# Row gathers with an explicit index bound and skipping, in a two-layer graph network on one core

## Chip, cores and metric

The kernel runs on one core of a Trainium2 chip. The metric is the device time of one execution in microseconds (us), lower is better. TensorE is called PE in the rows (PEld is its weight load), VectorE DVE, ScalarE ACT, GpSimd POOL and SyncE SP.

## What is computed

Two graph layers on 6,250 nodes of 256 features and 206,250 directed edges sorted by destination. The first one is the part that gathers:

```python
h = relu(layernorm(x))
h_all = einsum('ni,roi->rno', h, weight)            # 8 relations
x = x + segment_sum(h_all[edge_type, src], dst) + bias
h = relu(layernorm(x))
hw = h @ W
out = segment_sum(dinv[src] * dinv[dst] * hw[src], dst) + b
x = x + leaky_relu(out, 0.2)
```

The kernel sums the rows `h[src]` per destination and relation first and multiplies by the relation's weights afterwards, which is the same sum in another order.

## The kernel before

**Prologue.** The rows of `h` are written to `table0` in HBM, 50 tiles of 128 rows (6,400 rows; node i is row i + 64, the rest are padding). The edges are laid out in chunks of 128: `idxT` holds one column of 128 source rows for every chunk, one index per partition. An index is a source node plus 64, so the largest is 6,313; a padded place holds 64. A count of edges that fit the fast layout is compared with E, and the fast path, `both_layers`, runs; the other path, `aggregate_any`, is not executed with these inputs.

**First layer.** A chunk is fetched by one indirect DMA on GpSimd (L1116): 128 rows of 1 KB from `table0` into `rows`. Three chunks make a lot, 538 lots in all (1,612 chunks), and `rows` is a ring of `RING0` = 7 lots. In `sum_lot`, TensorE waits until a lot's rows have landed and multiplies them with one-hot matrices that ScalarE makes (L1657, 12 matmuls for a lot); its last matmul raises `s_pe`, and GpSimd waits on that before it issues the gathers of the lot seven later. After every tile come the projections by the relation weights (L1673).

**Between the lots.** A plan written into the program gives TensorE other work after each lot: counts of edges for the second layer (L1687, up to some 1,300 us), and the dense products of the second layer (L1719). ScalarE and VectorE prepare their operands. GpSimd's queue holds little besides the row gathers: `look` (one gather of `records` at L1097, behind a wait of its own at L1096) and `fetch` (four gathers at L1104), seven times each, and at the end 46 direct DMAs that add to the output (L1125). So GpSimd's order is a single stream of 1,647 indirect DMAs, 1,612 of them of rows.

Of the kernel before, what the change touches and what calls it, by code (L numbers as in the profile page):

```python
# [4 lines left out]
P = 128  # L5
LOT = 3
# [796 lines left out]
def both_layers(nc, D, V):  # L803
# [5 lines left out]
    R, NB, DF, DF3, T, SEGS = D.rel, D.nb, D.d, 3 * D.d, D.tiles, D.segs  # L809
# [10 lines left out]
    idxT, iota, iota4, ident, identb, dinv, ps_slot, ps_proj, ps_aux = (  # L820
        V[k] for k in ("idxT", "iota", "iota4", "ident", "identb", "dinv", "ps_slot", "ps_proj", "ps_aux"))
# [9 lines left out]
    with ExitStack() as ctx:  # L831
# [3 lines left out]
        def sem(name):  # L835
            return ctx.enter_context(nc.semaphore(f"f_{name}"))
# [79 lines left out]
        s_rows = [sem(f"rows{k}") for k in range(RING0)]  # L916
# [45 lines left out]
        def chunks_of(n):  # L962
            return min(LOT, D.chunks - LOT * n)
# [44 lines left out]
        def parts_stored(t):  # L1008

            return [sum(16 if k >= D.batch[-1][0] else 32 for k in range(i, t + 1, 2)) for i in range(2)]  # L1010
# [47 lines left out]
        def out_rows(t):  # L1058

            if t == 0:  # L1060
                return V["out"][0:HALF, :], HALF, P
            if t == T - 1:
                return V["out"][D.n - D.last_rows:D.n, :], 0, D.last_rows
            return V["out"][t * P - HALF:(t + 1) * P - HALF, :], 0, P
# [22 lines left out]
        @block.gpsimd  # L1087
        def _(eng):
            eng.iota(iota_m[:, :], [[int(FAR), PAIR], [1, T]], base=0, channel_multiplier=0,
                     allow_small_or_imprecise_dtypes=True).then_inc(s_iota, 1)  # L1090

            def look(b):

                if b > 0:
                    eng.wait_ge(s_kw, 2 * b)
                eng.wait_ge(s_first, b + 2)  # L1096
                eng.indirect_dma_start(recs[:, :], None, V["records"],  # L1097
                                       bass.IndirectOffsetOnAxis(ap=firstx[:, b:b + 1], axis=0)).then_inc(s_look[b % 2], 16)

            def fetch(b):  # L1100

                eng.wait_ge(s_off, b + 1)
                for i in range(SPAN):
                    eng.indirect_dma_start(recs[:, i * 2 * P:(i + 1) * 2 * P], None, V["records"],  # L1104
                                           bass.IndirectOffsetOnAxis(ap=record[:, i:i + 1], axis=0)).then_inc(s_rec, 16)

            for n in range(PL.nlot):
                if n in PL.look:
                    look(PL.look[n])
                if n in PL.fetch:  # L1110
                    fetch(PL.fetch[n])
                k = n % RING0
                if n >= RING0:
                    eng.wait_ge(s_pe, n - RING0 + 1)
                for c in range(chunks_of(n)):
                    eng.indirect_dma_start(rows0[:, k, c, :], None, V["table0"],  # L1116
                                           bass.IndirectOffsetOnAxis(ap=idxT[:, n * LOT + c:n * LOT + c + 1], axis=0)).then_inc(s_rows[k], 16)
            def add_to_out(k):

                t = PL.order[k]  # L1120
                eng.wait_ge(s_lk, k + 1)
                for i in range(2):
                    eng.wait_ge(s_st[i], parts_stored(t)[i])
                rows_out, a, b = out_rows(t)
                eng.dma_start(rows_out, hh[a:b, k % NOUT, :], accum_op=ALU.add).then_inc(s_o[k % NOUT], 16)  # L1125

            for k in range(T - DIRECT):
                add_to_out(k)
# [996 lines left out]
```

## Time and profile before

| | |
|---|---|
| time, median of 3 runs | 2742.73 us (2742.18 to 2746.72) |
| span of the profiled execution, first to last instruction | 2254.7 us |
| outside the span (median less span) | 488.0 us |
| mean granted TensorE clock | 0.956 |
| first and last row gather issued | 59.1 us and 2136.4 us |

The profile gives no separate time for the profiled execution, so its span is set beside the median of the runs: 488.0 us of the time lie outside what the profile calls the span. The stretch of the row gathers takes 92% of the span. TensorE is the busiest engine (88%), then GpSimd and ScalarE (72% and 71%).

### The profile page before, as it was taken

The page shows a single profiled execution, that of the slowest core. Times are in us where ns is not written, and L with a number is a line of the kernel's source. Part 1 is how long each engine was busy: PE and PEld are TensorE (multiplying, and loading weights), DVE is VectorE, ACT ScalarE, POOL GpSimd, SP SyncE. Part 2 cuts the span into 40 slices and gives each one's busy share as a digit, 9 for nine tenths or more (in the row PEclk, how much of TensorE's full clock was granted, in tenths as well). Part 3 has the DMA queues.
Part 4 walks back from the last instruction along what each step waited for, and adds up shares of the span by engine and source line. Part 5 has one row for each costly group of instructions (what it writes and reads, how often), then busy time and mean ns, then how long its engine had stood idle before and what let it go on. Part 6 is the DMA issues. An engine that isn't in the chain of part 4 may idle for free.

```text
span 2254.7 us, 45577 instructions
## 1 busy us (share of the span) xinstructions
PE 1992.8 (88%) x14761; PEld 1803.1 (80%) x14761; DVE 1276.9 (57%) x3614; ACT 1609.8 (71%) x3919; POOL 1623.6 (72%) x1721
## 2 busy tenths in 40 slices
PE   1467887888988898878999999999999999999998
PEld 1467777878878787767888899898988898889877
DVE  7466666658667666856776653333233234454567
ACT  6646687678878688777888887767767768686631
POOL 2777777777777777777777677777777777777625
PEclk7788998989999999889999999999999999999999
DMA  9434556555656665565675567655556556666656
GB/s 306 154 117 141 152 159 183 154 152 173 192 177 178 204 173 148 165 184 161 211 208 169 176 182 256 193 157 166 164 150 183 149 153 166 156 167 154 146 87 91
DMA packets 371502, 381.11 MB, mean 169 GB/s; under 512 B 242815, under 2 KB 292288, under 8 KB 371136
## 3 DMA queue, kind: packets, MB, share of 16 engines
q0 software_dynamic: 85392, 221.49, 34.8%
q1 hardware_dynamic: 240336, 111.41, 18.3%
q10 hardware_dynamic: 45536, 45.26, 6.1%
q8 instruction: 122, 2.00, 0.4%
q14 instruction: 116, 0.95, 0.1%
HBM read 301.20 MB, written 76.81 MB: 168 GB/s over the span
## 4 chain that ended last, share of the span: by engine, by line
PE 61%; POOL 16%; ACT 8%; issue 7%; DMA 3%; DVE 2%; ACTq 1%; DVEq 0%; POOLq 0%
PE ps_slot L1657 21%; POOL rows_f L1116 15%; PE ps_slot L1719 13%; PE ps_proj L1673 12%; PE ps_aux L1719 9%; PE ps_slot L1687 3%; DMA rows_f<-table,idxT 3%; ACT staged_f L1298 2%; ACT gap_f L1363 2%; PE ps_slot L1764 1%; ACT wide_f L1356 1%; POOL recs_f L1104 1%; ACT onehot_f L1371 1%; ACT acc_f L1284 1%; DVE hots_f L1546 0%
## 5 line engine op out<-in xcount | busy, mean ns | idle before, releaser
L1116 POOL DMA_INDIRECT rows_f<-table,idxT x1612 | 1535.3, 952 | 498.9 <-issue 472.5
L1657 PE MATMUL ps_slot<-onehot_f,rows_f 128*128 128x128 f32 x6448 | 858.2, 285 | 139.7 <-DMA rows_f<-table,idxT 114.8
L1657 PEld LDWEIGHTS ps_slot<-onehot_f,rows_f 128*128 128x128 f32 x6448 | 813.6, 198 | 173.5 <-DMA rows_f<-table,idxT 128.2
L1363 ACT ACTIVATE gap_f<-iota,keyT 128x128 bf16<-128x128 bf16 x1614 | 527.5, 395 | 70.0 <-ACT staged_f L1298 47.7
L1298 ACT ACTIVATE staged_f<-ps_slot 128x400 uint8<-128x400 f32 x800 | 345.7, 500 | 170.5 <-PE ps_slot L1687 170.3
L1543 DVE TENSOR_TENSOR hots_f<-ps_slot,keys_f 128x400 bf16<-128x400 bf16 x800 | 285.4, 357 | 292.4 <-PE ps_slot L1687 291.8
L1673 PE MATMUL ps_proj<-w0t,acc_f 128*128 128x256 f32 x1600 | 367.0, 383 | 0.9 <-DVE xt_f L1461 0.7
L1371 ACT ACTIVATE onehot_f<-gap_f 128x384 f32<-128x384 bf16 x538 | 277.3, 515 | 119.0 <-PE ps_slot L1657 118.6
L1356 ACT ACTIVATE wide_f<-abuf_f 128x512 fp32r<-128x512 uint8 (+1 forms) x488 | 270.0, 611 | 100.5 <-PE ps_slot L1719 70.9
L1673 PEld LDWEIGHTS ps_proj<-w0t,acc_f 128*128 128x128 f32 x1600 | 301.0, 193 | 39.4 <-issue 1.1
L1546 DVE TENSOR_TENSOR hots_f<-ps_slot,keys_f 128x512 bf16<-128x512 bf16 x800 | 329.9, 412 | 0.0
L1448 DVE TENSOR_TENSOR acc_f<-ps_slot,acc_f 128x256 f32 x538 | 226.8, 422 | 172.4 <-PE ps_slot L1657 105.1
L1719 PE MATMUL ps_slot<-wide_f,stash_f 128*128 128x512 f32 (+1 forms) x1276 | 315.8, 390 | 1.8 <-DVE sums_e_f L1576 1.8
L1719 PE MATMUL ps_aux<-wide_f,stash_f 128*128 128x512 f32 (+1 forms) x1168 | 305.2, 405 | 0.0
L1719 PEld LDWEIGHTS ps_slot<-wide_f,stash_f 128*128 128x128 f32 x1276 | 222.5, 189 | 42.0 <-DVE sums_e_f L1576 2.0
L1687 PE MATMUL ps_slot<-hots_f 128*128 128x100 bf16 x3200 | 213.1, 211 | 47.9 <-ACT staged_f L1298 27.5
L1719 PEld LDWEIGHTS ps_aux<-wide_f,stash_f 128*128 128x128 f32 x1168 | 214.1, 194 | 40.5 <-issue 0.3
L1687 PEld LDWEIGHTS ps_slot<-hots_f 128*128 128x128 bf16 x3200 | 188.7, 115 | 68.9 <-issue 33.2
L1576 DVE TENSOR_TENSOR sums_e_f<-ps_slot,sums_e_f 128x512 f32<-128x512 f32 x105 | 72.0, 690 | 154.0 <-PE ps_slot L1719 153.5
L1576 DVE TENSOR_TENSOR sums_e_f<-ps_aux,sums_e_f 128x512 f32<-128x512 f32 x87 | 59.7, 686 | 79.1 <-PE ps_aux L1719 78.8
L1284 ACT ACTIVATE acc_f<-ident 128x2048 f32<-128x2048 f32 x52 | 99.6, 1916 | 5.6 <-PE ps_proj L1673 5.6
L1356 ACT ACTIVATE wide_f<-keys_f 128x512 fp32r<-128x512 uint8 (+1 forms) x147 | 78.2, 583 | 16.5 <-PE ps_slot L1719 16.3
(169 smaller groups left out, 1015.4 us busy)
## 6 DMA issues: line engine op xcount, KB each, us to landing
rows_f<-table,idxT POOLq DMA_INDIRECT x1612
abuf_f<-counts_d SPq DMA_DIRECT2D x70, 320.0 KB
stash_f<-table SPq DMA_DIRECT2D x14, 1280.0 KB, 8.6
table<-hs_f SPq DMA_DIRECT2D x47, 256.0 KB
table<-xres SPq DMA_DIRECT2D x10, 640.0 KB, 6.8
xt_f<-in_x_dram SPq DMA_DIRECT2D x48, 128.0 KB
out_dram<-xt_f SPq DMA_DIRECT2D x48, 128.0 KB
out_dram<-acc_f POOLq DMA_DIRECT2D x45, 128.0 KB, 3.4
```

Source lines behind the costliest of these rows:

```text
L1116: eng.indirect_dma_start(rows0[:, k, c, :], None, V["table0"], bass.IndirectOffsetOnAxis(ap=idxT[:, n * LOT + c:n * LOT + c + 1], axis=0)) ...
L1298: eng.activation(staging[:, h % 2, :, (w % HSUB) * SUB:(w % HSUB + 1) * SUB], count_bank(w)[:, 0:SPAN * MW].rearrange("p (d t) -> p t d", ...
L1356: eng.activation(wide_of(i, u).rearrange("p (h c) -> p h c", c=HW), counts, ACT.Copy).then_inc(s_wide, 1)
L1363: last = eng.activation(gap[:, n % 2, c, :], iota[:, :], ACT.Abs, scale=-1.0, bias=V["key"][:, n * LOT + c:n * LOT + c + 1])
L1371: eng.activation(onehot[:, n % HOTS, :, :], gap[:, n % 2, :, :], ACT.Relu, scale=-1.0, bias=1.0).then_inc(s_oh, 1)
L1448: eng.tensor_tensor(win, part, win, ALU.add).then_inc(s_acc, 1)
L1543: eng.tensor_tensor(hot_m[:, w % NHOT, :, :].rearrange("p s (m q) -> p s m q", q=2), m_numbers.rearrange("p (m q) -> p m q", q=2).unsqueez ...
L1546: eng.tensor_tensor(hot_lo[:, w % NHOT, :, :], lo_numbers, lo_e[:, b % 2, k, :].unsqueeze(1).to_broadcast([P, P, SPAN]), ALU.is_equal).the ...
L1657: last = eng.matmul(o[:, b * W:(b + 1) * W], rows0[:, k, c, b * P:(b + 1) * P], onehot[:, n % HOTS, c, :], start=(c == 0), stop=(c == chun ...
L1673: last = eng.matmul(ps_proj[:, 0:DF], acc[:, b * R + r, a:a + P], V["w0t"][:, r, b, :], start=(r == 0 and b == 0), stop=(r == R - 1 and b ...
L1687: last = eng.matmul(o[:, j * MW:(j + 1) * MW], hot_lo[:, w % NHOT, :, j], hot_m[:, w % NHOT, j, :], start=True, stop=True)
L1719: last = eng.matmul(o, stash_of(k)[:, t, p * DF + half * P:p * DF + (half + 1) * P].bitcast(f32r), wide_of(w, u), start=(t == 0 and p == 0 ...
```

## The change

Every row gather gets a bound for its indices, 6399 (`T * P - 1`, the last row of `table0`), and the flag that an index beyond it is skipped; before, there was no bound given and the flag said that a bad index is an error. The gathers of `records` stay as they are.

```diff
                 for c in range(chunks_of(n)):
                     eng.indirect_dma_start(rows0[:, k, c, :], None, V["table0"],
-                                           bass.IndirectOffsetOnAxis(ap=idxT[:, n * LOT + c:n * LOT + c + 1], axis=0)).then_inc(s_rows[k], 16)
+                                           bass.IndirectOffsetOnAxis(ap=idxT[:, n * LOT + c:n * LOT + c + 1], axis=0),
+                                           bounds_check=T * P - 1, oob_is_err=False).then_inc(s_rows[k], 16)
```

In the built program each of the 1,612 gathers differs in this way (printed from the program; fields that are the same on both sides are left out):

```
before:
  PSEUDO_DMA_DIRECT2D  dge_op=INDIRECT1D ...
  PSEUDO_EXTENSION     mode=SRC_INDIRECTION idx_bound_is_err=1 ...
after:
  MOVE                 dtype=int32 $R[8]=6399
  PSEUDO_DMA_DIRECT2D  dge_op=INDIRECT1D ... src_bound_reg=$R[8]
  PSEUDO_EXTENSION     mode=SRC_INDIRECTION src_bound_size_bytes=6553600 ...
```

## Rows read from the trace of the kernel before

**Rows 1.** The page, its span and busy time (share of the span).

```profile
span 2254.7 us, 45577 instructions
PE 1992.8 (88%) x14761; PEld 1803.1 (80%) x14761; DVE 1276.9 (57%) x3614; ACT 1609.8 (71%) x3919; POOL 1623.6 (72%) x1721
```

**Rows 2.** The page, chain that ended last, by engine and line.

```profile
PE 61%; POOL 16%; ACT 8%; issue 7%; DMA 3%; DVE 2%; ACTq 1%; DVEq 0%; POOLq 0%
```

**Rows 3.** Groups of instructions, GpSimd: busy us, mean ns, idle before, releasers.

```profile
L1116 POOL DMA_INDIRECT rows_f<-table,idxT x1612 | 1535.3, 952 | 498.9 <-issue 472.5 <-PE ps_slot L1657 26.3
L1104 POOL DMA_INDIRECT recs_f<-records,record_f x28 | 27.4, 979 | 8.5 <-issue 8.5
L1097 POOL DMA_INDIRECT recs_f<-records,firstx_f x7 | 6.6, 945 | 2.1 <-issue 2.1
```

**Rows 4.** Timeline of GpSimd near 300 us: start, duration, idle before.

```profile
299.54 0.95 POOL L1116 DMA_INDIRECT rows_f<-table,idxT  x1 [0.31 <-issue]
...
329.58 0.94 POOL L1116 DMA_INDIRECT rows_f<-table,idxT  x1 [0.30 <-issue]
```

**Rows 5.** TensorE's longest waits, 59 to 1000 us: total, times, longest.

```profile
PE ps_slot L1657 <- DMA rows_f<-table,idxT: 114.8, 60, 7.4
PE ps_slot L1657 <- DVE acc_f L1448: 20.6, 9, 9.0
```

**Rows 6.** TensorE's longest waits, 1000 to 1320 us.

```profile
PE ps_slot L1687 <- ACT staged_f L1298: 14.3, 10, 2.8
PE ps_slot L1687 <- ACT keys_f L1309: 5.2, 2, 3.8
```

**Rows 7.** Busy time by stretch: length, engines (busy, count), clock, DMA share, GB/s.

```profile
59.00:1000.00 941.00, 770.42 (x6776) 709.51 (x6775) 622.99 (x1895) 688.03 (x1729) 714.11 (x745) 0.92 0.56 166
1320.00:2140.00 820.00, 820.00 (x5112) 736.72 (x5112) 315.16 (x730) 594.69 (x1418) 618.71 (x653) 1.00 0.61 169
```

**Rows 8.** L1116 alone, 59 to 1000 us: length, POOL busy (count), clock, DMA.

```profile
59.00:1000.00 941.00, 684.79 (x715) 0.92 0.56 166
```

**Rows 9.** TensorE's timeline near the last gather that it waits for.

```profile
985.99 2.93 PE L1657 MATMUL ps_slot<-onehot_f,rows_f 128*128 128x128 f32 x12 [2.28 <-DMA rows_f<-table,idxT]
...
993.18 2.08 PE L1657 MATMUL ps_slot<-onehot_f,rows_f 128*128 128x128 f32 x8 [3.56 <-DMA rows_f<-table,idxT]
```

**Rows 10.** GpSimd's timeline in the same place.

```profile
982.67 0.95 POOL L1116 DMA_INDIRECT rows_f<-table,idxT  x1 [0.30 <-issue]
...
986.43 0.95 POOL L1116 DMA_INDIRECT rows_f<-table,idxT  x1 [0.30 <-issue]
```

**Rows 11.** GpSimd's waits, 1240 to 1320 us.

```profile
POOL rows_f L1116 <- issue: 16.1, 53, 0.3
POOL rows_f L1116 <- PE ps_slot L1657: 9.3, 6, 2.5
```

**Rows 12.** GpSimd's last gathers, then TensorE's last full lot (timeline).

```profile
2135.16 0.94 POOL L1116 DMA_INDIRECT rows_f<-table,idxT  x1 [0.30 <-issue]
2136.40 0.94 POOL L1116 DMA_INDIRECT rows_f<-table,idxT  x1 [0.30 <-issue]
...
2139.82 1.50 PE L1657 MATMUL ps_slot<-onehot_f,rows_f 128*128 128x128 f32 x12
```

**Rows 13.** Line L1096, the sequencer's own waits: ns min/median/max, first to last start.

```profile
L1096 POOLq EVENT_SEMAPHORE  x6: 17/17/17, 134.8 to 1080.1; - x6
```

**Rows 14.** GpSimd's timeline: the gathers that stand behind first and last such wait.

```profile
150.11 0.94 POOL L1097 DMA_INDIRECT recs_f<-records,firstx_f  x1 [0.30 <-issue]
...
1085.62 0.94 POOL L1097 DMA_INDIRECT recs_f<-records,firstx_f  x1 [0.30 <-issue]
```

**Rows 15.** Line L316 in the prologue, two MOVEs and what they load for.

```profile
L316 POOLq MOVE  x2: 29/29/29, 3.3 to 3.4; - x2
L316 POOL TENSOR_SCALAR_AFFINE_SELECT ident<-ident x1: 293/293/293, 3.4 to 3.4; 128x128 f32<-128x128 f32 x1
L316 POOL TENSOR_SCALAR_AFFINE_SELECT identb<-identb x1: 293/293/293, 3.7 to 3.7; 128x128 bf16<-128x128 bf16 x1
```

**Rows 16.** Line L1116 over 59 to 2140 us: ns min/median/max, first to last start.

```profile
L1116 POOL DMA_INDIRECT rows_f<-table,idxT x1612: 941/947/1799, 59.1 to 2136.4; - x180
```

## Prediction

> **What bounds the kernel now.** I read the page first. By busy share TensorE is the bound: 88% against GpSimd's 72% [rows 1], and the chain that ended last gives TensorE 61% and GpSimd 16% [rows 2]. Both are averages over stretches with different limits, so I went by stretch.
>
> GpSimd's groups come next. The 1,612 row gathers take 952 ns each, and of the 498.9 us idle before them 472.5 us are "issue", in which GpSimd waits for nothing that the profile shows [rows 3]. The timeline says what that is: from 299.54 to 329.58 us lie 24 steps, so a gather starts every (329.58 - 299.54) / 24 = 1.252 us, 0.95 generating and 0.30 between [rows 4]. From 59.1 to 2136.4 us the engine issues 1,647 gathers [rows 3, 16], so 2077.3 / 1646 = 1.262 us each. The stream never pauses for long: GpSimd is used up although its busy share says 72%.
>
> Whether its pace counts is read from who waits for rows. Up to 1000 us TensorE waits 114.8 us in 60 waits for them, its largest wait [rows 5]; there the gathers set the time. The last two of these waits end at 985.99 and 993.18 us [rows 9]. From 1000 to 1320 us it waits for ScalarE's copies instead [rows 6], gathers run ahead until the ring is full, and GpSimd is made to wait for TensorE: 9.3 us in 6 waits, each with the usual 0.30, so 7.5 us more than the cadence [rows 11]. From 1320 to 2140 us TensorE is busy 820.00 of 820.00 us [rows 7]; it is the bound and waits for no row.
>
> That second stretch has little room, though. The last full lot starts at 2139.82 us and its last gather was issued at 2135.16, the one before the single-chunk lot's [rows 12]: 4.66 us. The lot that started at 985.99 us, having waited, had its last gather at 982.67: 3.32 us [rows 9, 10]. So 1.3 us of lead are left at the end of the stream.
>
> **How a change of the cadence becomes time.** Let a row gather take d ns more. The last wait for rows belongs to the gather issued at 986.43 us [rows 9, 10]. In 59 to 1000 us there are 715 row gathers [rows 8], ten of them start after 986.43 at 1.252 us each, so 705 stand up to it, and the time moves by 0.705 d us. Behind it TensorE has its own pace until the lead is gone. The 7.5 us that GpSimd waits near 1240 to 1320 us swallow what the some 230 gathers in between add ((1270 - 986) / 1.25), up to d = 33 ns. From 1320 us on there are 653 row gathers [rows 7], which eat the 1.3 us at d = 2 ns. So the loss is 0.705 d + (0.653 d - 1.3) for d from 2 to 33, and 0.230 d - 7.5 more beyond 33. If d is negative, only the first term acts: the gain is 0.705 us a nanosecond at first and can't pass the 114.8 us that TensorE waits for rows.
>
> A measurement of this kernel can tell about 0.2% from no change, 5.5 us. That is d = 5.0 ns of 1,252 on the slow side and 7.8 ns on the fast side. The question is therefore what one gather costs to a few nanoseconds.
>
> **Edit 1, the 1,612 MOVEs.** A MOVE of this sequencer takes 29 ns [rows 15]. 1,612 of them would be 46.7 us of sequencer time in a row. I take them at nothing, since the sequencer is far ahead of the cores: the wait at L1096 stands right before the L1097 gather in the program, and it was done at 134.8 us where that gather started at 150.11, and the last at 1080.1 for 1085.62 [rows 13, 14]. So 5.5 to 15.3 us of generation, 4 to 12 gathers, lie queued in front. For each gather's 1.252 us the sequencer has one gather and one MOVE to handle. The prologue shows the same with registers: both MOVEs of L316 are done at 3.3 and 3.4 us, the second's own instruction starts at 3.7, so a register's value is taken without waiting for the instruction ahead to end [rows 15]. The cover is the queue; if it were gone, a MOVE would cost 29 ns or, with its dispatch, up to the some 0.1 us between the two in rows 15.
>
> The page Perfetto Trace Analysis of the Trainium skill, section on the GpSimd DMA instruction, says that the sequencer pushes the instruction into a wait queue and is then ready to decode the next; the lead just read agrees. The page DMA: Bandwidth & Descriptors, section on the anatomy of a GpSimd DMA, puts sequencer dispatch at about 50 ns; if each MOVE paid that in line, the formula would give 35.3 + 31.4 + 4.0 = 71 us, an estimate from that page, and this change would be a clear loss. By the rows it is nothing.
>
> **Edit 2, the bound itself.** The cores get a bound and compare 128 indices with it, or compared them before against something that never fails. No gather of this trace carries a bound. From below: nothing, if the comparison is already made with no bound given. What speaks for that: before, the flag said that a bad index is an error, so the path that handles an index has a branch for it. Also, the cost looks insensitive to what is asked: rows of 1 KB, rows of 2.5 KB and of 512 B generate in about the same time, 952, 945 and 979 ns mean [rows 3], with a minimum of 941 and a median of 947 for row gathers [rows 16]. From above: 1,252 ns over 128 indices is 9.8 ns an index; if a compare and a branch add a tenth of that to every index, d is 125 ns. In between stands a check that is made for many indices at once, which I size at 5 to 40 ns. Between ends of 0 and 125 ns I take 0, the end that the flat cost by shape is nearest to, with little confidence.
>
> **Edit 3, skipping instead of reporting.** No index is beyond the bound (largest 6,313), so nothing is skipped and every transfer stays: 128 rows of 1 KB. The two modes may run different code. From above on the fast side, the 0.30 us between two gathers could shrink if it held handling of errors; half of it, 150 ns, would be worth about 100 us, where the waits for rows run out. From the other side the skipping path may keep an account of how many descriptors are left, which falls into the range of edit 2. I take nothing.
>
> **Sum.** 0 + 0 + 0 on the profiled 2254.7 us, beside which 488.0 us lie outside the span; the sum stands for 2742.73, the median. With the smallest positive costs I write 2743.
>
> **Rivals.**
> Slower by the check (chance 0.34): the cores' generation of each gather grows from 0.95 us. With d = 20 ns the formula gives 14.1 + 11.8 = 26 us, 2769; with 40 ns 28.2 + 24.8 + 1.7 = 55 us, 2797; with 125 ns 88.1 + 80.3 + 21.3 = 190 us, 2932. For it: a gather with a bound names one thing more to be done, and 5 ns are enough to be seen. Against it: the flat 942 to 947 ns.
> Slower by the MOVE (0.05): it falls into the 0.30 us between gathers. At 29 ns 20.4 + 17.6 = 38 us, 2781; at 0.1 us 70.5 + 64.0 + 15.5 = 150 us, 2893. Against it: the lead in rows 13 and 14.
> Slower outside the span (0.03): 488.0 us over 45,577 instructions is 10.7 ns each; 1,612 more would be 17 us, 2760, if that part went by their number, of which the trace says nothing.
> Faster (0.16): the path that skips is shorter than the one that reports. With 20 ns the gain is 14 us, 2729; with 60 ns it is 42 us, 2701. It counts from 7.8 ns on.
> No change that can be told (0.42): d between -7.8 and +5.0 ns, 2735 to 2748 with the outer noise. This is the likeliest.
>
> **Range.** The likeliest case alone reaches from 2737 to 2748. For 8 in 10 I go to d = 42 ns on the slow side, 29.6 + 26.1 + 2.2 = 58 us, so 2800, and to 25 ns on the fast side, 18 us, so 2725. Left out are costly checks and MOVEs in line (about 0.12) and larger gains (about 0.07). Chances: faster 0.16, same 0.42, slower 0.42.
>
> **What would show it.** In the changed kernel's profile: the step from gather to gather (1.252 us now) and the two parts of it, 0.95 and 0.30. A MOVE in line shows in the 0.30, a check in the 0.95. TensorE's waits for rows should stay at 114.8 us before 1000 us and none after 1320 us; if d is above 2 ns, such waits appear near 2100 us, and GpSimd's 7.5 us near 1240 to 1320 us shrink. MOVE rows at L1116 should run several gathers ahead. The prediction is wrong if the step changes by more than some 5 ns, or if the span stays and the time moves.

## The result, and the profile after

The changed kernel takes 2783.27 us (median, 2778.82 to 2786.27, 4 runs), the kernel before beside it 2744.72 us (2742.18 to 2747.82, 4 runs): a ratio of 1.0135 with a 95% interval of 1.0121 to 1.0149, 38.6 us slower. That is in the range, on the side to which the text gave as much chance (0.42) as to its forecast of no change. That it lies in the range is luck, as the last part shows.

The profile of the changed kernel holds a surprise that goes before everything else. Its page, with busy time and the chain that ended last:

```profile
span 2784.4 us, 47189 instructions
PE 2218.3 (80%) x14761; PEld 1929.3 (69%) x14761; DVE 1277.2 (46%) x3614; ACT 1633.7 (59%) x3919; POOL 1709.8 (61%) x1721
...
PE 61%; issue 12%; ACT 11%; another core or an unknown queue 7%; DVE 4%; POOL 2%; ACTq 1%; DMA 0%; DVEq 0%; POOLq 0%
```

The span, 2784.4 us, is nearly the profiled run's time, 2786.0. Before, 2254.7 stood beside 2742.73 [rows 1], and I had put 488 us "outside the span". Nothing of this size lies outside: in every profiled run below, the span is within 2 us of its own time. The unchanged kernel takes 2251 us on two of the chips used and 2707 us on two others, and each chip kept its rate throughout. So the first trace and the first times probably came from different chips; their chips aren't on record. In what follows chip A is one on which before takes about 2250 us (two different chips), chip B one on which it takes about 2707 (again two), and chip C the one of the result (2744.72). Every ratio is between runs on the same chip; where a kernel on one chip B is compared with a kernel on the other, the text says so.

GpSimd's groups after, to be set beside [rows 3], then line L1116 alone, beside [rows 16]:

```profile
L1116 POOL DMA_INDIRECT rows_f<-table,idxT x1612 | 1621.0, 1006 | 918.8 <-issue 425.3
```

```profile
L1116 POOLq MOVE  x1612: 29/29/29, 58.7 to 2655.1; - x180
L1116 POOL DMA_INDIRECT rows_f<-table,idxT x1612: 995/1002/1788, 59.5 to 2655.8; - x180
```

The 1,612 MOVEs are there, 29 ns each. A gather takes 1002 ns (median) instead of 947: the bound costs 55 ns, and it lies in the engine's own 0.95 us. The timeline of the same kernel:

```profile
302.48 1.00 POOL L1116 DMA_INDIRECT rows_f<-table,idxT  x1 [2.50 <-remote]
303.79 1.00 POOL L1116 DMA_INDIRECT rows_f<-table,idxT  x1 [0.30 <-issue]
```

The 0.30 us between two gathers [rows 4] hasn't changed. But on this chip there are stops like the 2.50 us ("remote" stands for a releaser that the profile could not name). Idle before L1116 sums to 918.8 us, where 1,612 steps of 0.304 would make 490: GpSimd stands still for 429 us beyond its cadence. The gathers, which set the pace in the trace of before, do not set it here.

### The profile page after: what moved, and what is told of

Same layout as the page of the kernel before. It is cut to its first block, busy times and chain, and to the rows that moved or that the text cites. A ratio compares the mean times of both kernels' runs of the same rounds, so it can differ in the third digit from the quotient of the medians.

```text
span 2784.4 us, 47189 instructions
## 1 busy us (share of the span) xinstructions
PE 2218.3 (80%) x14761; PEld 1929.3 (69%) x14761; DVE 1277.2 (46%) x3614; ACT 1633.7 (59%) x3919; POOL 1709.8 (61%) x1721
## 4 chain that ended last, share of the span: by engine, by line
PE 61%; issue 12%; ACT 11%; another core or an unknown queue 7%; DVE 4%; POOL 2%; ACTq 1%; DMA 0%; DVEq 0%; POOLq 0%
PE ps_slot L1658 22%; PE ps_proj L1674 12%; PE ps_slot L1720 11%; PE ps_aux L1720 8%; PE ps_slot L1688 6%; ACT staged_f L1299 3%; ACT gap_f L1364 3%; POOL rows_f L1116 2%; ACT onehot_f L1372 1%; ACT wide_f L1357 1%; PE ps_slot L1765 1%; PE ps_aux L1797 1%; DVE hots_f L1547 1%; DVE hots_f L1544 1%
## 5 line engine op out<-in xcount | busy, mean ns | idle before, releaser
L1116 POOL DMA_INDIRECT rows_f<-table,idxT x1612 | 1621.0, 1006 | 918.8 <-issue 425.3
L1658 PE MATMUL ps_slot<-onehot_f,rows_f 128*128 128x128 f32 x6448 | 961.1, 298 | 181.5 <-issue 118.6
L1658 PEld LDWEIGHTS ps_slot<-onehot_f,rows_f 128*128 128x128 f32 x6448 | 889.3, 210 | 236.8 <-issue 173.6
L1299 ACT ACTIVATE staged_f<-ps_slot 128x400 uint8<-128x400 f32 x800 | 357.7, 500 | 468.7 <-remote 304.4
L1674 PE MATMUL ps_proj<-w0t,acc_f 128*128 128x256 f32 x1600 | 390.7, 395 | 28.4 <-issue 27.0
L1688 PE MATMUL ps_slot<-hots_f 128*128 128x100 bf16 x3200 | 251.5, 220 | 199.5 <-ACT staged_f L1299 95.2
L1720 PE MATMUL ps_slot<-wide_f,stash_f 128*128 128x512 f32 (+1 forms) x1276 | 346.2, 407 | 45.6 <-issue 33.4
L1688 PEld LDWEIGHTS ps_slot<-hots_f 128*128 128x128 bf16 x3200 | 205.1, 118 | 246.2 <-issue 213.3
L1449 DVE TENSOR_TENSOR acc_f<-ps_slot,acc_f 128x256 f32 x538 | 227.2, 422 | 297.4 <-remote 146.1
L1720 PE MATMUL ps_aux<-wide_f,stash_f 128*128 128x512 f32 (+1 forms) x1168 | 329.8, 425 | 20.7 <-issue 19.2
L1720 PEld LDWEIGHTS ps_aux<-wide_f,stash_f 128*128 128x128 f32 x1168 | 226.8, 206 | 73.7 <-issue 28.5
```

Of the source, the lines that this page charges most:

```text
L1299: eng.activation(staging[:, h % 2, :, (w % HSUB) * SUB:(w % HSUB + 1) * SUB], count_bank(w)[:, 0:SPAN * MW].rearrange("p (d t) -> p t d", ...
L1449: eng.tensor_tensor(win, part, win, ALU.add).then_inc(s_acc, 1)
L1658: last = eng.matmul(o[:, b * W:(b + 1) * W], rows0[:, k, c, b * P:(b + 1) * P], onehot[:, n % HOTS, c, :], start=(c == 0), stop=(c == chun ...
L1674: last = eng.matmul(ps_proj[:, 0:DF], acc[:, b * R + r, a:a + P], V["w0t"][:, r, b, :], start=(r == 0 and b == 0), stop=(r == R - 1 and b ...
L1688: last = eng.matmul(o[:, j * MW:(j + 1) * MW], hot_lo[:, w % NHOT, :, j], hot_m[:, w % NHOT, j, :], start=True, stop=True)
L1720: last = eng.matmul(o, stash_of(k)[:, t, p * DF + half * P:p * DF + (half + 1) * P].bitcast(f32r), wide_of(w, u), start=(t == 0 and p == 0 ...
```

## Experiments

### The kernel before again, the flag, the register, the MOVEs (chip B)

Before, beside all four: 2708.32 us (2699.92 to 2719.30, 21 runs).

**e0_before** is the kernel before, unchanged.

> The kernel before, unchanged, profiled again. Its profiled execution spanned 2254.7 us where its timed runs gave 2742 to 2748; the changed kernel's span is 2784.4 at a time of 2786.0. Theory A: the first profile of before fell on an execution 488 us shorter than the timed ones; now the span is within 5 us of the time, about 2742, GpSimd waits for TensorE for some 500 us in total, and a row gather still takes 947 ns. Theory B: 488 us really lie outside before's span and not outside after's; now the span is again about 2255 and the time about 2744.

2709.6 us, ratio 1.0007 (0.9988 to 1.0026), span 2711.8. Theory A holds, though at 2710 us and not at 2742: the span is the time. Its page, its gathers, and its busy time from 1320 to 2140 us (columns as in [rows 7]):

```profile
span 2711.8 us, 45577 instructions
PE 2181.5 (80%) x14761; PEld 1903.4 (70%) x14761; DVE 1280.9 (47%) x3614; ACT 1628.9 (60%) x3919; POOL 1621.7 (60%) x1721
...
L1116 POOL DMA_INDIRECT rows_f<-table,idxT x1612 | 1533.5, 951 | 932.0 <-issue 396.6
```

```profile
1320.00:2140.00 820.00, 718.90 (x4579) 622.15 (x4579) 309.15 (x865) 527.20 (x1264) 509.46 (x538) 0.95 0.52 153
```

A gather takes 951 ns as before; but TensorE is busy 719 of 820 us where the first trace had 820 [rows 7]. (The 820 us don't hold the same work in both: 538 row gathers here, 653 there.) GpSimd's idle time beyond the cadence is 932.0 - 490 = 442 us. Between the two spans, 2254.7 and 2711.8, lie 457 us with one and the same program: TensorE is busy 189 us longer (2181.5 against 1992.8) and idle 268 us longer, and the others follow. Its waits:

```profile
PE ps_slot L1687 <- issue: 130.2, 113, 4.0
PE ps_slot L1657 <- issue: 85.2, 132, 3.0
PE ps_slot L1687 <- ACT staged_f L1298: 76.1, 59, 6.8
PE ps_slot L1657 <- DMA rows_f<-table,idxT: 27.9, 10, 10.9
```

It waits 27.9 us for rows here, 114.8 up to 1000 us in [rows 5]; its largest waits are for nothing that the profile shows ("issue"). The releasers must be read with care on this chip: for the ring's first place the trace holds 985 events of landed rows, where the trace of before holds 3,659. But rows aren't what is missing: a lot that TensorE starts without a wait had its last gather issued 24 us earlier (median), 14 us in the first trace. The mean granted clock is 0.919 against 0.956, 4% lower where the span is 20% longer, so it can't be all of it.

**e1_err** gives the bound and reports an index beyond it:

```diff
-    bounds_check=T * P - 1, oob_is_err=False)
+    bounds_check=T * P - 1, oob_is_err=True)
```

> The bound is given, but an index beyond it is reported (the flag as before). Theory A, the bound costs: a gather takes 1002 ns in the trace and the time is that of the change, 2783 us (ratio 1.0135). Rival, the skipping costs: 947 ns and 2744 us (ratio 1.000). In between if both have a part.

2746.95 us, ratio 1.0151 (1.0127 to 1.0175). The loss doesn't hang on skipping. With the flag for reporting a gather is 1013 ns, so with a bound the skipping mode is the cheaper one, by some 11 ns:

```profile
L1116 POOL DMA_INDIRECT rows_f<-table,idxT x1612: 1007/1013/2004, 59.8 to 2614.7; - x180
```

**e2_onereg** is the change with the register loaded once:

```diff
+            bound = eng.alloc_register("row_bound")
+            eng.reg_mov(bound, T * P - 1)
             for n in range(PL.nlot):
...
-    bounds_check=T * P - 1, oob_is_err=False)
+    bounds_check=bound, oob_is_err=False)
```

> The change, with the register loaded once instead of ahead of each of the 1,612 gathers. Theory A, the MOVEs are hidden: 1002 ns a gather, 0.30 us between, 2783 us (ratio 1.0135). Rival, the MOVEs have a part in it: 947 to 990 ns or a shorter gap, and a ratio between 1.000 and 1.010.

2698.14 us, ratio 0.9969 (0.9950 to 0.9988). Neither theory had this: a gather still takes 999 ns (median), and the loss is gone.

```profile
L1118 POOL DMA_INDIRECT rows_f<-table,idxT x1612 | 1617.3, 1003 | 840.0 <-issue 404.5
```

The idle time fell from 932.0 to 840.0 us, 92, while the work of the gathers grew from 1533.5 to 1617.3, 84. On this chip the bound is paid out of GpSimd's idle time. So the 52 ns (947 to 999) are the bound's, and the loss of time on this chip is the MOVEs', or something that comes with them.

**e3_moves** was to have the MOVEs alone:

```diff
                 for c in range(chunks_of(n)):
+                    eng.reg_mov(bound, T * P - 1)
```

> The kernel before, with a MOVE of 6399 into an unused register ahead of each row gather and no bound. Theory A, MOVEs are free: 947 ns a gather, 1.252 us from gather to gather, ratio 1.000. Rival, they cost by themselves: up to 29 ns each, 47 us or less, ratio up to 1.017.

2707.94 us, ratio 1.0003 (0.9990 to 1.0016), but the page shows 45,577 instructions, as before, and the trace holds no MOVE at these lines: nothing reads the register, and the MOVEs were left out of the program. The run says nothing on its question and is a repeat of before.

### What it is about the MOVEs

Printing the changed program where a lot begins shows what I had missed:

```
before:  PSEUDO_DMA_DIRECT2D $S[179]>=4 ...
after:   MOVE $S[179]>=4 dtype=int32 $R[8]=6399
         PSEUDO_DMA_DIRECT2D ... src_bound_reg=$R[8]
```

The wait of L1114 goes to the next instruction in the program. That was the gather; now it is the MOVE, the sequencer's own work. Four kernels tell this from the number of instructions. They ran on chip A (before 2250.83 us, 2247.86 to 2255.03, 23 runs).

**e4_move_first** keeps all MOVEs and the bound and puts the wait behind the first MOVE of a lot:

```diff
-                if n >= RING0:
-                    eng.wait_ge(s_pe, n - RING0 + 1)
                 for c in range(chunks_of(n)):
+                    eng.reg_mov(bound, T * P - 1)
+                    if c == 0 and n >= RING0:
+                        eng.wait_ge(s_pe, n - RING0 + 1)
...
-    bounds_check=T * P - 1, oob_is_err=False)
+    bounds_check=bound, oob_is_err=False)
```

> The change, with all 1,612 MOVEs and the bound, but each lot's wait for TensorE placed behind the first MOVE of the lot, so that the gather carries it and not the MOVE. Theory A, the loss of 1.35 to 1.5% comes from the MOVE that carries the wait: ratio 0.997 to 1.000, as with one register load in all, and a gather starts 258 ns after TensorE's signal. Rival, the loss comes from 1,612 more instructions to fetch and run: ratio 1.013 to 1.015 as in the change.

2331.12 us, ratio 1.0353 (1.0340 to 1.0366). Outside both, since both spoke of chip B.

**e5_move_a_lot** has 538 MOVEs, each with the lot's wait:

```diff
                 if n >= RING0:
                     eng.wait_ge(s_pe, n - RING0 + 1)
+                eng.reg_mov(bound, T * P - 1)
                 for c in range(chunks_of(n)):
...
-    bounds_check=T * P - 1, oob_is_err=False)
+    bounds_check=bound, oob_is_err=False)
```

> The change with one MOVE a lot (538 instead of 1,612), and that MOVE carries the lot's wait. Theory A, the wait on the MOVE: the whole loss, ratio 1.013 to 1.015. Rival, the number of instructions: a third of it, 1.005 or less.

2330.73 us, ratio 1.0351 (1.0338 to 1.0364). With a third of the MOVEs and the wait back on them the time is that of e4: on chip A neither matters, the bound does.

**e6_seq_wait** is before with the wait on an empty sequencer instruction:

```diff
                     eng.wait_ge(s_pe, n - RING0 + 1)
+                    eng.nop(nofuse=True)
```

> The kernel before, no bound and no MOVE, but the lot's wait stands on an empty instruction of the sequencer in front of the gather. Theory A, what costs is that the sequencer itself waits: ratio 1.013 to 1.015, and a held gather starts some 0.7 us after TensorE's signal instead of 0.26. Rival, it takes the register with the wait: ratio 1.000.

2252.80 us, ratio 1.0005 (0.9994 to 1.0015). On this chip few gathers are held, so it doesn't decide what a waiting sequencer costs on chip B. Its trace does decide the delay, though on only three held lots (at 1270.0, 1298.3 and 1314.0 us): the empty instruction starts 0.023 us after TensorE's signal, and the gather 0.737 to 0.738 us after it, with no MOVE, register or bound. In the first trace a held gather starts 0.26 us after the signal. So the rival, that it takes the register, is out for the delay.

**e7_ring6** is before with `RING0 = 6`.

> The kernel before with a ring of six lots instead of seven, so that every held gather comes a whole lot (about 5 us) later, by a wait that still stands on the gather. Theory A1, the loss comes from gathers that start 0.5 us later: here ten times that delay, ratio well above 1.015. Theory A2, late gathers cost nothing since TensorE hardly waits for rows (28 us in all), and the loss is something else that the waiting sequencer does: ratio 1.000 to 1.005.

2251.91 us, ratio 1.0004 (0.9995 to 1.0013): a lot less in the ring costs nothing on chip A. With so few held gathers it tells neither of its two theories from the other. GpSimd's waits for TensorE sum to no more than with seven [rows 3]:

```profile
POOL rows_f L1116 <- issue: 472.8, 1551, 0.6
...
POOL rows_f L1116 <- PE ps_slot L1657: 24.5, 61, 2.5
```

**e8_after** is the change, on chip A too (before 2252.25 us, 2249.13 to 2254.92, 9 runs, for this and e9).

> The change once more, since before runs at 2251 us on one chip and at 2708 and 2744 on two others. If this is a chip of the fast kind (before near 2250): the gathers set the pace up to 1000 us and at the end, each takes 54 ns more, and the formula of the prediction gives 77 us, ratio 1.034 to 1.035, the same as with the wait on the gather. If it is a chip of the slow kind (before near 2700 or more): ratio 1.0135 to 1.015 as measured.

2332.53 us (2331.14 to 2334.61), ratio 1.0358 (1.0343 to 1.0372). This is the run that can be set beside the rows of before, since both have GpSimd going nearly without a stop. Its page, chain and gathers; two steps of the timeline; and TensorE's waits for rows up to 1000 us and from 1380 to 2210 us:

```profile
span 2329.5 us, 47189 instructions
...
PE 41%; POOL 29%; issue 12%; ACT 7%; DMA 6%; DVE 2%; POOLq 1%; ACTq 1%; DVEq 0%
```

```profile
L1116 POOL DMA_INDIRECT rows_f<-table,idxT x1612 | 1617.2, 1003 | 491.9 <-issue 465.7 <-PE ps_slot L1658 26.2
```

```profile
299.54 1.00 POOL L1116 DMA_INDIRECT rows_f<-table,idxT  x1 [0.30 <-issue]
...
330.80 1.00 POOL L1116 DMA_INDIRECT rows_f<-table,idxT  x1 [0.30 <-issue]
```

```profile
PE ps_slot L1658 <- DMA rows_f<-table,idxT: 130.3, 63, 7.1
```

```profile
PE ps_slot L1658 <- DMA rows_f<-table,idxT: 24.7, 23, 3.4
```

The step is (330.80 - 299.54) / 24 = 1.303 us instead of 1.252, d = 51 ns. The prediction's formula gives 36.0 + 32.0 + 4.2 = 72 us; the spans differ by 2329.5 - 2254.7 = 74.8, the medians by 80.3. Its signs are there as well: GpSimd's stops near 1240 to 1320 us are gone (86 waits for TensorE of 0.30 us each, 26.2 in all), TensorE waits for rows up to 1000 us for 130.3 us instead of 114.8 [rows 5], and behind 1380 us, where it never waited, for 24.7. The chain that ended last gives GpSimd 29% where it gave 16% [rows 2].

**e9_move_first** is the kernel of e4 beside it.

> All 1,612 MOVEs and the bound, the lot's wait carried by the gather. On a chip of the fast kind: 1.035, as before. On a chip of the slow kind, theory A (the MOVE that carries the wait costs): 0.995 to 1.000, since the bound alone gave 0.997 there. Rival (the number of MOVEs costs): 1.013 to 1.015, like the change beside it.

2330.77 us, ratio 1.0349 (1.0335 to 1.0363), its interval over that of e8. On chip A the place of the wait makes no difference that can be told.

### The deciding pair (chip B)

Before 2706.88 us (2699.61 to 2716.80, 23 runs).

**e10_onereg** is the kernel of e2.

> The bound with one register load in all, again. On a chip of the fast kind (before near 2250): the 53 ns are in the bound and not in the MOVEs, so 1.034 to 1.036 as with 1,612 MOVEs. On a chip of the slow kind: 0.995 to 0.999 as before.

2702.10 us, ratio 0.9982 (0.9967 to 0.9998).

**e11_move_first** is the kernel of e4.

> All 1,612 MOVEs and the bound, the wait carried by the gather. On a chip of the slow kind, theory A (the MOVE that carries the wait costs): the same as one register load, 0.995 to 1.000. Rival (the number of MOVEs): 1.013 to 1.015. On a chip of the fast kind: 1.035 a third time, which leaves the cause on the slow kind open.

2711.57 us, ratio 1.0011 (0.9996 to 1.0025). 1,612 MOVEs and the bound, and the loss is gone as soon as the gather carries the wait: theory A. The MOVE carrying it had cost 1.0151 on the other chip B (e1) and 1.0135 on chip C; the changed kernel itself was not run beside e11. What ties the two chips B together is the kernel with one register load, which gives 0.9969 on one and 0.9982 on the other. The MOVEs may not be wholly free: e11 is 9.5 us (0.35%) slower than e10 on the same chip, a quarter of the loss. What the wait's place does, in rows: the MOVEs and gathers from 300.5 us on, first of the changed kernel (chip C) in 300.5 to 302.6 us, where the gather was held for 2.50 us, then of e11 in 300.5 to 301.3, where one was held for 0.97.

```profile
L1116 POOLq MOVE  x2: 29/29/29, 301.7 to 302.3; - x2
L1116 POOL DMA_INDIRECT rows_f<-table,idxT x1: 1000/1000/1000, 302.5 to 302.5; - x1
```

```profile
L1115 POOLq MOVE  x1: 29/29/29, 300.9 to 300.9; - x1
```

```profile
L1118 POOL DMA_INDIRECT rows_f<-table,idxT x1: 996/996/996, 301.2 to 301.2; - x1
```

In the change the held gather's own MOVE comes at 301.7 us and the gather 0.73 us after that. In e11 its own MOVE ran at 297.4 us, before the hold; the one at 300.9 us belongs to the next gather. The trace's semaphore events show the same for held lots in general; one each, in us, near 355 to 365 us (`s_pe` is TensorE's signal):

```
             engine free   s_pe raised   own MOVE   gather starts   after the signal   next gather's MOVE
change           363.431       364.429    364.453         365.186              0.757              364.969
e11              354.952       356.190    352.005         356.449              0.259              356.222
e0 (before)      354.563       355.399          -         355.656              0.257                    -
```

The sequencer stands still in both: in e11, too, the next gather's MOVE comes only 0.032 us after the signal (in 266 of 274 held lots). What differs is on which side of the wait the gather is handled. After a hold the MOVEs follow each other by 0.516 us, so that is what the sequencer spends on one gather and one MOVE. A gather that waits itself has been handled before the signal and starts 0.26 us after it. With the wait on the MOVE, the MOVE runs 24 ns after the signal, the gather is handled only then, and starts 0.73 us after the MOVE. 226 of the 531 lots with a wait are held so in the changed kernel.

On TensorE's side one group of waits goes with the loss: those before the matmuls with the rows that have no releaser. From e1 and e2, which ran on the same chip, then from e11 and the change:

```profile
PE ps_slot L1658 <- issue: 113.7, 197, 1.7
```

```profile
PE ps_slot L1660 <- issue: 84.6, 128, 3.7
```

```profile
PE ps_slot L1660 <- issue: 62.8, 109, 1.7
```

```profile
PE ps_slot L1658 <- issue: 118.6, 180, 2.6
```

Most of it lies between the twelve matmuls of one lot, and TensorE waits for rows only ahead of the first of them. These stops inside a lot sum to 84, 81, 70, 76 and 56 us in the profiles without the loss (e0, e3, e2, e10, e11), to 111 and 117 us in the two with it (e1 and the change), and to 0.0 us in the first trace and in e6, e7, e8 and e9 on chip A. One profile each, but the difference, 41 us between e1 and e2 and 27 to 61 over all pairs, is of the size of the loss.

## Why the prediction came out as it did

**What bounds the kernel** was read rightly for the chip of that trace and wrongly for the chip of the time. On chip A the gathers pace the first 1000 us and the formula for a slower gather fits (72 us by the formula, 75 by the spans, 80 by the medians). On B and C TensorE is slower, GpSimd has some 440 us to spare, and on B 84 us of added work vanish in it. The sentence that failed is the one that took 488.0 us as lying "outside the span": that difference was the sign that the trace did not stand for the time.

**Edit 2, the bound**, was taken at 0 between ends of 0 and 125 ns; it measures 51 to 55. By the prediction's own sign, a step that changes by more than some 5 ns, it was wrong. The flat cost by row size [rows 3] was no evidence, as none of those gathers had a bound. On chip A this mis-sized term is the whole result, 3.5%; on B it costs nothing (0.9969 and 0.9982, both intervals just below 1). With the measured 55 ns the formula would have put the result at 2743 + 38.8 + 34.6 + 5.2 = 2822 us, beyond the range; 2783 lies inside because on chip C the bound isn't what costs.

The lead of 1.3 us at the end of the stream was a soft term as well. It takes the 3.32 us of one lot as what a lot needs behind its last gather, but the other lot of the same rows had its last gather issued at 986.43 and started at 993.18, 6.75 us later [rows 9, 10]. On chip A the waits for rows begin again well before 2100 us (24.7 us of them from 1380 us on).

**Edit 3**: against the flag for reporting, the skipping flag saves some 11 ns of a gather that has a bound (one profile of each); it is small beside the bound. Skipping is not why the kernel got slower (e1).

**Edit 1, the MOVEs "at nothing"**, is the step that failed for the stated result. Their own 29 ns are hidden for the most part, as argued: e11, with 1,612 of them, is at 1.0011, and 9.5 us above e10, where 29 ns each in line would be 47 us. But I wrote that no wait was added or taken away and did not see that a wait changed hands: from the gather, which the sequencer has handled by then, to a MOVE ahead of it, so that the gather is handled only after the signal. The lead of the sequencer over the cores [rows 13, 14] is there on chip A, up to 12 gathers, and it ends at every wait that isn't met yet. I had the rival "slower by the MOVE" with another mechanism (29 ns or more in the 0.30 us between gathers); that gap did not move. Its 38 us, the sum for 29 ns in line, is the measured loss by accident.

The page Perfetto Trace Analysis of the Trainium skill, section on the GpSimd DMA instruction, says that the instruction is pushed into a wait queue and that the sequencer is then ready for the next, before the semaphores are satisfied. That the gather is handled before its wait ends agrees with e11 (0.26 us after the signal). That the sequencer goes on meanwhile doesn't: its next MOVE comes 0.032 us after the signal, and the measurement decides.

**Open.** That the loss on chips like B goes with the wait's place is shown by e11, across two chips of one kind; that it is the same on C is inferred. The way from gathers that start 0.5 us late to TensorE isn't shown. TensorE waits for rows little more than before (37.0 us in the changed kernel, 27.9 in e0, 38.1 in e11), and the loss builds up evenly over the lots. The time shows up as stops inside lots whose rows have landed, and nothing in the traces says what a late gather, or a sequencer that waits at a MOVE, has to do with them. No run tested a sequencer's wait without MOVEs on chip B. Open, too, is why TensorE is slower there at all: with the same instructions, its largest waits have no releaser in the profile.

No version beats before on both kinds of chip. One register load gains 0.2 to 0.3% on B; on A, where it wasn't run, the bound is there with its 52 ns and the kernels that have it lose 3.5%.

## What to carry to other kernels

A span far from the measured time is not time outside the kernel until one profile with its own time has shown it. Ask whether trace and time come from the same chip, since what bounds the kernel, and with it the price of a change, can differ. An argument that takes a constant by register brings a register load ahead of the instruction, and a wait written before both lands on the load: load once, or load ahead of the wait. An option on a software-made gather is paid on every gather, needed or not; where the gathers are the bound, 50 ns of 1,250 are 3.5% of the time.

## What the runs showed that was not expected

- A bound on the indices lengthens the generation of a gather of 128 rows from 947 to 1002 ns if bad indices are skipped, and to 1013 ns if they are reported.
- A held gather starts 0.26 us after the signal if it carries the wait, 0.74 to 0.76 us if a sequencer instruction ahead of it does (an empty one in e6, a MOVE in the change). In both cases the sequencer gets no further until the signal.
- The sequencer spends 0.516 us on one gather and its MOVE.
- The same program takes 2251, 2708 or 2745 us on different chips, with gather and ScalarE times alike (951 and 952 ns a gather; ScalarE 1628.9 and 1609.8 us busy). TensorE stops inside lots for 84 us in e0, and for 0.0 us in the first trace.
- A ring of six lots instead of seven costs nothing on chip A (1.0004).
